# Mixture of experts in a two-layer kernel: every token through every expert, against sorted tiles of chosen rows moved by indirect DMA

## What is computed

```python
gate_logits = nx @ gate_W
topk_vals, topk_idx = jax.lax.top_k(gate_logits, TOP_K)          # TOP_K = 2 of 8 experts
gate_w = jax.nn.softmax(topk_vals, axis=-1)
dense_gates = jnp.sum(jax.nn.one_hot(topk_idx, N_EXPERTS) * gate_w[..., None], axis=-2)
for e in range(N_EXPERTS):
    h = jax.nn.gelu(jnp.einsum('bsd,fd->bsf', nx, fc1_w[e]) + fc1_b[e])     # 128 -> 512
    y = jnp.einsum('bsf,df->bsd', h, fc2_w[e]) + fc2_b[e]                   # 512 -> 128
    moe_out = moe_out + y * dense_gates[..., e:e + 1]
```

## Time and profile before

| what | value |
|---|---|
| median of 3 runs | 1288.93 us (1286.11 to 1290.6) |
| profiled execution | 1292.51 us |
| its span, first to last instruction | 1290.7 us |
| mean granted PE clock | 0.964 |
| busy: PE / DVE / ACT / POOL | 1147.6 / 874.0 / 746.6 / 313.3 us |
| mixer, attention | to about 240 us, then to about 718 us |
| experts | 718 to 945 us |
| scan, net | 945 to 1150 us, 1150 to 1290 us |

### The profile page before, as it was taken

The page is one execution under the profiler, slowest core; times in us unless marked ns, Lnnn a source line. Parts: engine busy times, 40 slices in busy tenths (PEclk is TensorE's granted clock), DMA queues, the critical chain, the costliest instruction groups (busy, mean ns, idle before and its releaser), DMA issues.

```text
span 1290.7 us, 15518 instructions
## 1 busy us (share of the span) xinstructions
PE 1147.6 (89%) x5584; PEld 573.3 (44%) x5584; DVE 874.0 (68%) x1660; ACT 746.6 (58%) x1116; POOL 313.3 (24%) x260
## 2 busy tenths in 40 slices
PE   5799777888999999999999999999968889779998
PEld 2455443433333333333322565655523334347776
DVE  4788658958888888878843443444369999964443
ACT  5677532455665565646688544445658676435554
POOL 4323321210010000000011300000079788830000
PEclk9889889999999999989999999999989899889999
DMA  5210553344000000000000312211132223100000
GB/s 163 82 56 29 164 122 82 91 107 92 2 2 2 2 1 1 1 1 2 1 27 10 112 43 60 87 41 33 34 114 107 86 111 115 66 0 1 9 9 17
DMA packets 30491, 67.25 MB, mean 52 GB/s; under 512 B 3816, under 2 KB 16112, under 8 KB 28368
## 3 DMA queue, kind: packets, MB, share of 16 engines
q1 hardware_dynamic: 30416, 66.27, 17.7%
HBM read 57.47 MB, written 8.78 MB: 51 GB/s over the span
## 4 chain that ended last, share of the span: by engine, by line
PE 56%; DVE 15%; POOL 10%; issue 9%; ACT 9%; DMA 1%; SPq 0%; DVEq 0%; POOLq 0%; ACTq 0%
PE psum L1620 8%; PE psum L1328 8%; PE psum L1213 7%; PE psum L1282 6%; POOL drive L2055 6%; DVE mx L1225 6%; PE psum L386 5%; PE psum L388 5%; PE psum L387 5%; DVE hst L2077 2%; ACT probs L1296 2%; ACT psum L2015 1%; ACT edec L615 1%; PE psum L528 1%; PE psum L381 1%
## 5 line engine op out<-in xcount | busy, mean ns | idle before, releaser
L1225 DVE TENSOR_REDUCE mx<-psum 128x1 f32<-128x512 f32 (+3 forms) x640 | 349.2, 604 | 64.7 <-PE psum L1213 35.4
L1296 ACT ACTIVATE probs<-psum 128x1024 f32<-128x1024 f32 (+1 forms) x320 | 283.5, 936 | 171.7 <-PE psum L1282 151.3
L1213 PE MATMUL psum<-kz,qa 128*128 128x512 bf16 (+3 forms) x640 | 199.6, 354 | 22.6 <-DVE mx L1225 16.3
L1282 PE MATMUL psum<-qa,kz 128*128 128x512 bf16 (+1 forms) x640 | 174.9, 361 | 7.2 <-DMA qa<-m_rows 4.2
L1328 PE MATMUL psum<-probs,v 128*32 128x512 f32 (+3 forms) x1280 | 151.3, 544 | 1.5 <-POOL probs L1307 1.4
L1638 DVE TENSOR_TENSOR hid<-hid,gate_bc 128x1024 f32<-128x1024 f32 x64 | 79.0, 1241 | 106.7 <-ACT hid L1630 105.0
L2055 POOL TENSOR_TENSOR drive<-du,b_bc 128x1024 f32<-128x1024 f32 x64 | 148.7, 2359 | 1.4 <-issue 1.4
L2006 PE MATMUL psum<-hst,ident 128*128 128x512 f32 x256 | 122.1, 622 | 21.9 <-DVE u L2095 14.1
L1213 PEld LDWEIGHTS psum<-kz,qa 128*128 128x128 bf16 x640 | 57.1, 97 | 186.1 <-DVE mx L1225 136.9
L1630 ACT ACTIVATE hid<-psum,cols 128x512 f32<-128x512 f32 x128 | 84.7, 689 | 75.5 <-PE psum L388 75.3
L2077 DVE TENSOR_TENSOR_SCAN hst<-psum,hlast,drive 128x512 f32<-128x512 f32 x96 | 115.1, 1263 | 8.4 <-ACT psum L2015 6.4
(11 more groups left out here) (285 smaller groups left out, 1687.8 us busy)
## 6 DMA issues: line engine op xcount, KB each, us to landing
b_bc<-b_rows SPq DMA_DIRECT2D x16, 1024.0 KB, 4.7
cs_bc<-cs_rows SPq DMA_DIRECT2D x16, 512.0 KB, 4.7
gate_bc<-gate_rows SPq DMA_DIRECT2D x32, 256.0 KB, 3.2
qk_part_rows<-qk_parts SPq DMA_DIRECT2D x48, 128.0 KB, 2.3
ew_raw<-experts_dram SPq DMA_DIRECT2D x8, 512.0 KB, 3.6
qa<-qk_part_rows SPq DMA_DIRECT2D x16, 192.0 KB, 5.3
kz<-qk_part_rows SPq DMA_DIRECT2D x16, 192.0 KB, 5.9
fw_raw<-net_dram SPq DMA_DIRECT2D x11, 256.0 KB, 2.7
```

The source lines that it names most:

```text
L1213: ins = pe.matmul(out[:, 0:w], qa[:, b, h // 2, i * P:(i + 1) * P], key_rows(h, c)[:, 0:w], start=True, stop=not last, skip_group_check=True)
L1225: dve.tensor_reduce(mx[:, 4 * i + h % 4, c:c + 1], fill_bank("mx", k, n)[:, 0:w], AX.X, ALU.max).then_inc(S["mx_read"], 1)
L1282: ins = pe.matmul(out[:, lo:], key_rows(h, kt // TPB)[:, kt % TPB * P:(kt % TPB + 1) * P], qa[:, b, h // 2, lo:], start=True, stop=not dia ...
L1296: act.activation(probs[:, st % 2, hh, :, lo:], s_pair[n % 2][:, :, lo:], ACT.Exp, scale=SCALE).then_inc(S["p_done"], 1)
```

## The change

Only chosen rows go through an expert. The layer-normed tokens stay as rows (`xrow`). Two sorts (blocks 0 to 2, and block 3; `route_sort_dve`, 16 small DVE operations behind two matmuls that count) give each of a token's two choices a place in a table of rows in DRAM, in which each expert's rows are padded to whole tiles of 256. 19 tiles hold the first sort and 11 the second whatever is chosen, 30 in all, and a table names the expert of each tile. POOL scatters each 128-token tile's rows to both places (32 indirect DMAs), gathers each tile's 516 KB of weights by the table (30), and gathers the results back in token order (32), which DVE multiplies with the gates and adds (`combine_dve`). SP brings a tile's rows in (128 KB) and its results out. For a tile PE turns the rows (two transposes), makes four up and four down matmuls in plain f32 of 256 columns, and turns the result. Routing is done earlier: blocks 0 to 2 from item 13 on. With no sums to hold in PSUM, banks 6 and 7 serve the scan front.

Softplus becomes relu(x) + ln(1 + exp(-|x|)) in both places, of functions that share one activation table; the last sum is DVE's. Table loads are fixed at fewer places: 38 in the program, 49 before. SP copies input rows over the whole row tables once, in item 9 (3.75 MB), so that padding holds numbers.

```diff
+SORTS = ((0, 3 * TPB), (3 * TPB, TPB))
+SORT_TILES = tuple((2 * P * n + NE * (RT - 1)) // RT for _, n in SORTS)
+N_TILES = sum(SORT_TILES)
+W_SLOTS, ROW_SLOTS = 5, 3
...
-                act.activation(dt[b % 2][:, :], pj(DTREP), ACT.Softplus, bias=C("dt_bias")).then_inc(S["pj_act"], 1)
+                if b >= 1:
+                    act.wait_ge(S["dt_done"], b)
+                o.did(act.activation(dta[:, :], pj(DTREP), ACT.Abs, bias=C("dt_bias")))
+                act.activation(dt[b % 2][:, :], pj(DTREP), ACT.Relu, bias=C("dt_bias"))
+                o.wait()
+                o.did(act.activation(dta[:, :], dta[:, :], ACT.Exp, scale=-1.0))
+                o.wait()
+                act.activation(dta[:, :], dta[:, :], ACT.Ln, bias=one[:, 0:1]).then_inc(S["pj_act"], 1)
...
+        ROUTE_FROM = 13
+        ROUTE_PE = {3: [("x", 0)], 4: [("lg", 0)], 5: [("x", 1)], 6: [("lg", 1)], 7: [("x", 2)], 8: [("lg", 2)], 10: [("sort", 0)]}
+        ROUTE_ACT = {3: [("nx", 0)], 5: [("nx", 1), ("ex", 0)], 7: [("nx", 2), ("ex", 1)], 9: [("ex", 2)]}
+        ROUTE_DVE = {1: [("stats", 0)], 2: [("apply", 0)], 3: [("stats", 1)], 4: [("top2", 0), ("apply", 1)], 5: [("stats", 2)],
+                     6: [("gates", 0), ("top2", 1), ("apply", 2)], 8: [("gates", 1), ("top2", 2)], 10: [("sort", 0), ("gates", 2)]}
...
+        def scatter_pool(pool, t, k):
+            pool.indirect_dma_start(out=xs_rows[t // (3 * TPB)][:, :], out_offset=bass.IndirectOffsetOnAxis(ap=slot_no[:, k, t:t + 1], axis=0),
+                                    in_=xrow_at(t), in_offset=None).then_inc(S["rows_moved"], 16)
+        def weights_pool(pool, j):
+            if j >= W_SLOTS:
+                pool.wait_ge(S["yT_done"], j - W_SLOTS + 1)
+            pool.indirect_dma_start(out=ew[:, j % W_SLOTS, :], out_offset=None, in_=a["experts"].rearrange("e p w -> (e p) w"),
+                                    in_offset=bass.IndirectOffsetOnAxis(ap=weight_no[:, j:j + 1], axis=0)).then_inc(w_in[j % W_SLOTS], 16)
+        def gather_pool(pool, b):
+            need = N_TILES if b == NB - 1 else SORT_TILES[0]
+            for n in range(2):
+                pool.wait_ge(y_out[n], 16 * len(range(n, need, 2)))
+            pool.wait_ge(S["rows_moved"], SCATTERED + 16 * 2 * TPB * b)
+            if b >= 2:
+                pool.wait_ge(S["moe_added"], b - 1)
+            for k in range(2):
+                for i in range(TPB):
+                    t = b * TPB + i
+                    pool.indirect_dma_start(out=y_rows[:, b % 2, k, i, :], out_offset=None, in_=ys_rows[b // (NB - 1)][:, :],
+                                            in_offset=bass.IndirectOffsetOnAxis(ap=slot_no[:, k, t:t + 1], axis=0)
+                                            ).then_inc(S["rows_moved"], 16)
+        def combine_dve(o, dve, b):
+            dve.wait_ge(S["x_mixed"], NB + b + 1)
+            dve.wait_ge(S["rows_moved"], SCATTERED + 16 * 2 * TPB * (b + 1))
+            for k in range(2):
+                for i in range(TPB):
+                    t = b * TPB + i
+                    ins = dve.scalar_tensor_tensor(x_tok[:, t, :], y_rows[:, b % 2, k, i, :], gsel[:, k, t:t + 1], x_tok[:, t, :],
+                                                   ALU.mult, ALU.add)
+                    if k == 0:
+                        o.did(ins)
+                if k == 0:
+                    o.wait()
+            ins.then_inc(S["moe_added"], 1)
+        def rows_in_sp(sp, j):
+            s, rows = TILE_AT_ROW[j]
+            sp.wait_ge(S["rows_moved"], 16 * 2 * sum(SORTS[s]))
+            if j >= ROW_SLOTS:
+                sp.wait_ge(S["xt_turned"], j - ROW_SLOTS + 1)
+            sp.dma_start(xin[:, j % ROW_SLOTS, :, :].rearrange("p n d -> p (n d)"),
+                         xs_rows[s][rows, :].rearrange("(p n) d -> p (n d)", n=2)).then_inc(cs_in[j % ROW_SLOTS], 16)
+        def rows_out_sp(sp, j):
+            s, rows = TILE_AT_ROW[j]
+            sp.wait_ge(S["ytok_done"], j + 1)
+            sp.dma_start(ys_rows[s][rows, :].rearrange("(p n) d -> p (n d)", n=2),
+                         ytok[:, j % 2, :, :].rearrange("p n d -> p (n d)")).then_inc(y_out[j % 2], 16)
...
+        def rows_up_pe(pe, j, chunks):
+            if 0 in chunks:
+                pe.wait_ge(S["xTr_done"], j + 1)
+                pe.wait_ge(w_in[j % W_SLOTS], 16 * (j // W_SLOTS + 1))
+            for m in chunks:
+                if j >= 2 and m % 2 == 0:
+                    pe.wait_ge(S["gelu_done"], FC * (j - 2) + m + 2)
+                pe.matmul(hid_bank(j, m), ew[:, j % W_SLOTS, m * P:(m + 1) * P], xTr[:, j % 2, :], start=True, stop=True,
+                          skip_group_check=True).then_inc(S["hid_filled"], 1)
+        def rows_down_pe(pe, j):
+            if j >= 1:
+                pe.wait_ge(S["yT_done"], j)
             for m in range(FC):
+                pe.wait_ge(S["gelu_done"], FC * j + m + 1)
+                ins = pe.matmul(bank[1][:, 0:RT], ew[:, j % W_SLOTS, (FC + m) * P:(FC + m + 1) * P], hid[:, j % 2, m, :],
+                                start=(m == 0), stop=(m == FC - 1), skip_group_check=True)
+            ins.then_inc(S["down_done"], 1)
...
+        MF_PE = {26: ("turn",), 27: ("x",), 28: ("z",), 32: ("db",), 33: ("dt",), 35: ("u",)}
+        MF_ACT = {26: ("apply", "hi"), 28: ("x", "z"), 29: ("tap",), 31: ("xc", "gate"), 32: ("db",), 33: ("dt",), 35: ("u",)}
+        MF_DVE = {25: (0, "stats"), 30: ("conv0",), 31: ("conv1",), 32: (1,), 34: ("dsum",), 35: ("du",)}
+        COMBINE_SCAN = {3: 2, 9: 3}
...
+            for k in range(N_ROUNDS):
+                if k < N_TILES:
+                    rows_up_pe(pe, k, (0, 1))
+                if k + 1 < N_TILES:
+                    rows_turn_pe(pe, k + 1)
+                if k < N_TILES:
+                    rows_up_pe(pe, k, (2, 3))
...
+                if 1 <= k < N_TILES + 1:
+                    rows_down_pe(pe, k - 1)
+                if 2 <= k < N_TILES + 2:
+                    rows_back_pe(pe, k - 2)
...
+            for k, kp in DIAG[18:20]:
+                causal_pool(pool, k, kp)
+            pool.wait_ge(S["blank_saved"], BLANK_SAVED)
+            pool.wait_ge(S["slots_done"], 2)
+            for t, k in SCATTERS[:6]:
+                scatter_pool(pool, t, k)
+            for k, kp in DIAG[20:22]:
+                causal_pool(pool, k, kp)
+            for t, k in SCATTERS[6:]:
+                scatter_pool(pool, t, k)
+            for j in range(W_SLOTS):
+                weights_pool(pool, j)
             for k, kp in DIAG[22:]:
                 causal_pool(pool, k, kp)
+            for j in range(W_SLOTS, 7):
+                weights_pool(pool, j)
             ln_pool(pool, 2 * NB + NB - 1)
             inner_pool(pool, NB - 1)
+            for j in range(7, 16):
+                weights_pool(pool, j)
+            pool.wait_ge(S["slots_done"], 4)
+            for t, k in SCATTERS_LAST:
+                scatter_pool(pool, t, k)
+            for j in range(16, 24):
+                weights_pool(pool, j)
+            gather_pool(pool, 0)
+            for j in range(24, 26):
+                weights_pool(pool, j)
+            scan_front_pool(o, pool, 0, "ln")
+            for j in range(26, N_TILES):
+                weights_pool(pool, j)
+            for b in range(1, NB):
+                gather_pool(pool, b)
...
+            elif part == "dsum":
+                dve.wait_ge(S["c_ln_done"], b + 1)
+                for m in range(2):
+                    dve.scalar_tensor_tensor(delta[:, b % 2, m, :], scan_bank("dt", b, m)[:, :], 0.0, delta[:, b % 2, m, :],
+                                             ALU.max, ALU.add).then_inc(S["c_dt_read"], 1)
...
```

663 lines of the change are left out of this document (340 added, 323 removed).

## The result

The changed kernel took 1313.91 us (median of 4 runs, 1306.02 to 1323.5), the kernel before 1288.78 beside it: a ratio of 1.020, 95% interval 1.013 to 1.027. It is slower, by some 1 to 3%, where 1255 was forecast. Run again on another occasion, the same file took 1287.23 us (10 runs, 1283.24 to 1290.5) beside 1289.55: 0.998, interval 0.996 to 0.9995. So there are two questions: why it gains nothing even there, and what the other 27 us of the first runs are. The trace of the later occasion is used for the first, and is called the second trace.

The account below looks back on a forecast made before the run. PE's own arithmetic in the expert stage was taken as the bound (32 units x 6.17 = 197 us). Experts -48, attention +7, mixer +4, scan +4 gave -33 us: from 1292.5 to 1259.5, as a median 1255, range 1222 to 1290.

Parts of the forecast that it names:

- The expert stage: Attention's end to the scan's first drive: 179 us instead of 227, a gain of 48 us.
- Undisturbed rounds: One tile's round on PE in the expert stage: eight f32 matmuls and four transposes, 3.95 us; 30 rounds 118.5 us.
- An indirect DMA on POOL: POOL's time to issue one indirect DMA: taken as 1.3 us, with 0.8 to 2.4 kept possible.
- The wait ahead of tile 24: Expert stage: tile 24's weights stand behind block 0's eight gathers on POOL, so PE idles 5.7 us.
- that ahead of tile 26: Expert stage: tile 26's weights stand behind block 0's norm on POOL, so PE has nothing for 11 us.
- Attention: Routing moved into item 13: +10 us there, -3 in items 14 and 15, so +7; from nothing to +12.
- The 23 issues ahead of the last select: Attention's end: 18 scatters and 5 weight loads on POOL take 30 us, just covered by a gap of some 30.
- The mixer's term: Softplus of more steps, one table load less: about +1 us on each of four blocks' chains, +4, from 0 to +8.
- The scan's term: DVE's added combine and dsum steps, 10.9 us, mostly fit its gaps: scan +4 us, from 0 to +8.
- POOL's issues decide: Rival: costlier DMA issues on POOL delay attention and experts; at 2.0 us each 1290, at 2.3 1305; chance 0.13.
- item 13 longer with DVE busy: Sign in attention: item 13 at 47 us, with DVE full.
- a scan stage of over 215 us: Sign against the forecast: it is wrong if the scan is longer than 215 us.

Follow-up runs that it names:

- e6: Changed kernel with POOL issuing the weight gathers of tiles 26 to 28 ahead of the scan's norm of block 0; 1283.96 us (one run).
- e3: Changed kernel with softplus in the mixer as Exp and Ln alone, without Abs, Relu and DVE's add; 1303.45 us, ratio to before 1.009.
- e4: Changed kernel with combines of blocks 2 and 3 moved out of the scan's states, ahead of them; 1301.32 us, ratio to before 1.007.
- i2: The version with everything, unpaced, but POOL's first drive waits until block 3's combine is done; 1269.66 us, ratio to before 0.983.
- e1: Changed kernel with the 24 scatters of blocks 0 to 2 replaced by plain stores from SP's queue to fixed rows; 1291.12 us (one run).
- e5: Changed kernel with 24 scatters and 5 first weight gathers paced some 1.8 us apart instead of 1.26; 1281.85 us, ratio to before 0.993.
- g2: The paced scatters of e5 again, beside the changed kernel on the same chip; 1289.06 us, ratio to before 0.999.
- g1: The changed kernel itself, timed again in a later session; 1287.23 us, ratio to before 0.998.
- i1: The version with everything, unpaced, but block 3's combine back behind state 9 of block 0; 1272.86 us, ratio to before 0.986.
- control of the last session: The version with everything, unpaced and unchanged, run beside i1 and i2; 1276.02 us, ratio to before 0.990.
- h1: The changed kernel once more, as control of the fourth session; 1283.58 us (one run).
- e7: Changed kernel with the early combines of e4 and softplus in the scan as Exp and Ln alone; 1259.81 us, ratio to before 0.977.
- version with everything: Changed kernel with Exp and Ln softplus in mixer and scan, e4's early combines and e6's gather order; unpaced 1242.12 us, paced 1247.09.

## Why the prediction was wrong

The second trace's span is 27.8 us above the forecast one (1285.5 against 1257.7): 20.4 from the scan, 8.4 from the mixer, 1.4 from attention, less 2.5 from experts and rest. Two terms failed, and what no term had came on top in the first runs.

**The expert stage was right, nearly term by term.** Forecast 179 us, measured 177.5 (second trace). Undisturbed rounds repeat each 4.00 us in the traces (3.95 forecast). An indirect DMA on POOL takes 0.94 to 0.97 us by the medians and the next starts 1.25 to 1.27 us behind it (1.3 taken). The wait ahead of tile 24 was 4.6 to 5.0 us (5.7 forecast; the recorded terms 2.3 + 10.4 + 1.3 + 2.6 add to 16.6 and not to 17.7, and so to 4.6), that ahead of tile 26 10.8 (11). The traces don't name the weights as what ended these waits; that the second goes when the gathers are moved (e6) shows it for that one. From the first tile's matmul to the last it is 144.7 us (140 forecast as a sign, 149 by the sum's own terms), and 31.9 more to the first drive (28 forecast).

**Attention was right in sum, in part by luck**, +8.4 against +7, with its parts shifted. By the distance of the first select of an item's last steps from that of the item ahead, in the second trace:

```profile
601.21 1.23 POOL L1352 TENSOR_SCALAR_AFFINE_SELECT probs<-probs 128x512 f32<-128x512 f32 x2 [45.20 <-ACT probs L1341]
...
657.31 1.23 POOL L1352 TENSOR_SCALAR_AFFINE_SELECT probs<-probs 128x512 f32<-128x512 f32 x2 [1.27 <-ACT probs L1341]
...
700.26 1.23 POOL L1352 TENSOR_SCALAR_AFFINE_SELECT probs<-probs 128x512 f32<-128x512 f32 x2 [4.41 <-ACT probs L1341]
...
733.79 1.23 POOL L1352 TENSOR_SCALAR_AFFINE_SELECT probs<-probs 128x512 f32<-128x512 f32 x2
```

Item 13 takes 56.1 us (48.2 before, by the same rows), item 14 43.0 (38.0), item 15 33.5 (38.2): +7.9, +5.0 and -4.7, where +10, and -3 for the last two together, were forecast. The 23 issues ahead of the last select were covered.

**The mixer's term was mis-sized**: "Three more activations at 0.69 us, an add of the same size and handshakes, less 1.3, are about +1 us on each of four blocks' chains: **+4**". By its own numbers that is 3 x 0.69 + 0.69 - 1.3 = 1.5 before any handshake, and the handshakes were then rounded away. The second trace has +12.4 (+13.0 by the mean of 11 traces against the one trace before). The chain from a block's first activation to its decays is 1.8 to 1.9 us longer on each block, 7.4 together. Nor did the 1.3 us for the table load come back in block 0: without a load ahead its first activation starts at 17.0 us, after 1.1 us of waiting for PE, where it started at 15.65 behind the load. And e3, with Exp and Ln alone, brings 11.2 back by the means.

**The scan's term was wrong in kind**: "DVE ... gets 16 combine steps (0.4 us each) and six dsum steps (0.75): +10.9 us, most of it in its 22 us of gaps". Two things were missed. A combine step was priced without its neighbour: DVE's steps with two SBUF operands and POOL's drives shut each other out (14.0 us by e4; shown by i2). And dsum was counted as DVE time, where by the waits its cost is the banks that it holds: PE, ACT's decays and DVE's scans wait in turn (the whole of softplus is 14.8 us by e4 against i2; the share of the banks was not tested alone). The two make 28.8 us, the way from the changed kernel's scan to i2's, which is 4 us shorter than the one before the change; why it is shorter no run shows.

**What no term had** is the first runs' 27 us: long waits inside POOL's runs of transfers, 21.6 us in attention and some 5 in the experts. "POOL's issues decide" was the rival with this sign, but through the price of an issue, and that stayed at 1.26 us in both traces; nor was an issue stretched beside DVE, as that rival had it. Its mechanism was wrong too. e1 shows that in item 15 the waits need POOL's scatters or the long run that they make; what else they need is open.

Of the signs named in advance, four came (the round, the two waits, item 13 longer with DVE busy for 33.1 of 38 us) and POOL's rows stayed below 1.6 us. One that was to make the forecast wrong came as well: a scan stage of over 215 us (223 in the window above).

## What to carry to other kernels

When work is moved beside another engine's, price it by a row with the same pair of neighbours and the same kinds of operands, not by its own duration alone: a 0.35 us step took 2.4, and once 5.7. When a function is split into more steps, ask first which buffer stays taken longer and who waits for it; in the scan DVE waited 20.3 us for ACT's decays with the sum in place and 4.7 us without it. And time the changed kernel again beside every variant of it: e5 looked like a cure worth 30 us, and where its control stood beside it (g2, g1) it gave nothing.

## What the runs showed of the hardware

- A DVE step of 128x128 with both tensor operands in SBUF: 0.34 us alone, up to 2.44 us beside back-to-back POOL drives of 2.36 us, and once, in i1, 5.72 us; DVE steps with one operand in PSUM (0.68 and 1.16 us) were not stretched.
- An indirect DMA of 128 rows is 0.94 to 0.97 us of POOL by the medians and 1.25 to 1.27 us from one to the next, nearly the same for 512 B and for 4 KB rows.
- In some sessions, on two chips at least, ACT, DVE and PE stood inside or just behind runs of such DMAs for semaphores of work long done, ACT up to 15.2 us at a time (i1). In the control of the last session (ACT, 680 to 760 us):

```profile
ACT probs L1334 <- remote: 12.9, 2, 12.4
```

  In other sessions the changed kernel (g1, h1) and, on one of these two chips, kernels with the same run of scatters (e6, e7) had no such wait. It cost 27 us of the changed kernel (1313.9 against 1287.2) and some 30 of the version with everything (1276.0 against 1242.1 to 1245.6). With the rows stored by SP it was gone from attention and stayed in the experts (e1). Its cause is not settled.
- In the first trace PE's granted clock was 0.57 from 718 to 745 us, where it was busy 12.3 of 27 us, and 0.50, which is 1.2 GHz, from 720 to 740. Eight values matmuls took 1.94 us there and 1.07 ahead of the waits, so part of each long wait is paid twice.
